# Causal attention: two query groups of equal work and four column tiles instead of two query halves and two column tiles

## The reference

```python
Q, K, V = (proj(Wq, bq), proj(Wk, bk), proj(Wv, bv))
scores = jnp.einsum('bhqd,bhkd->bhqk', Q, K) / scale
scores = jnp.where(causal[None, None], -jnp.inf, scores)
attn = jax.nn.softmax(scores, axis=-1)
ctx = jnp.einsum('bhqk,bhkd->bhqd', attn, V)
out = jnp.einsum('bsd,ed->bse', ctx, Wo) + bo
```

## Time and profile before

| | us |
|---|---|
| median of 3 runs | 1139.42 |
| lowest, highest | 1137.17, 1140.31 |
| the profiled execution | 1135.98 |
| its span, first to last instruction | 1134.4 |

### The profile page before, as it was taken

One profiled execution on the slowest core, in us unless ns is written; L12 is line 12 of the kernel. 1 busy time (PEld: TensorE's weight loads), 2 busy tenths in 40 slices (PEclk: granted clock), 3 DMA queues, 4 the chain that ended last, 5 costly groups with the idle time before them and its releaser, 6 DMA issues.

```text
span 1134.4 us, 18322 instructions
## 1 busy us (share of the span) xinstructions
PE 864.2 (76%) x6048; PEld 506.0 (45%) x6049; DVE 552.8 (49%) x1051; ACT 387.5 (34%) x627; POOL 490.1 (43%) x538
## 2 busy tenths in 40 slices
PE   3199917277978847994689999758688855899995
PEld 1056603122222223662457777523334433577774
DVE  5623345467686352335513333458489755233334
ACT  3322202044455412221145555226402121555551
POOL 2228848888810021212234443123588731444431
PEclk9999957588798967996579999859899975899997
DMA  8224335655510010102843333230000044434323
GB/s 299 68 61 121 114 99 183 207 169 179 174 37 13 2 38 24 34 19 71 323 133 120 130 119 107 93 125 1 0 1 0 1 193 172 142 116 134 116 88 126
DMA packets 45580, 117.72 MB, mean 104 GB/s; under 512 B 10273, under 2 KB 23346, under 8 KB 44626
## 3 DMA queue, kind: packets, MB, share of 16 engines
q0 software_dynamic: 19280, 69.09, 19.1%
q1 hardware_dynamic: 21634, 43.64, 10.8%
q10 hardware_dynamic: 4608, 4.20, 1.1%
HBM read 90.16 MB, written 26.74 MB: 103 GB/s over the span
## 4 chain that ended last, share of the span: by engine, by line
PE 62%; DVE 15%; DMA 8%; POOL 5%; ACT 5%; issue 4%; SPq 1%; ACTq 0%; DVEq 0%; POOLq 0%
PE psum L490 18%; PE psum L518 13%; PE psum L1178 6%; PE psum L502 5%; PE psum L1638 4%; DVE mem L1272 2%; PE psum L174 2%; DMA mem<-w2l_dram 2%; PE psum L1153 2%; POOL mem L222 2%; DVE XTl L143 1%; PE psum L473 1%; PE psum L1665 1%; DMA max_dram<-mem 1%; ACT XTh L164 1%
## 5 line engine op out<-in xcount | busy, mean ns | idle before, releaser
L490 PE MATMUL psum<-mem 128*128 x984 | 233.3, 392 | 6.0 <-ACT psum L587 5.6
L518 PE MATMUL psum<-mem 128*128 x1536 | 178.2, 273 | 4.7 <-DVE mem L730 4.7
L518 PEld LDWEIGHTS psum<-mem 128*128 128x128 f16 x1536 | 149.9, 98 | 23.2 <-issue 5.6
L490 PEld LDWEIGHTS psum<-mem 128*128 128x128 f16 x984 | 98.8, 100 | 116.4 <-issue 20.4
L800 POOL DMA_INDIRECT y_dram<-mem x64 | 63.8, 997 | 164.5 <-DVE mem L738 161.7
L795 POOL DMA_INDIRECT mem<-xn_dram,mem x64 | 64.8, 1013 | 127.0 <-PE psum L473 109.5
L1230 ACT ACTIVATE mem<-psum 128x512 f32<-128x512 f32 (+1 forms) x160 | 80.0, 552 | 110.7 <-PE psum L1161 66.6
L1272 DVE TENSOR_REDUCE mem<-psum 128x2 f32<-128x1024 f32 (+2 forms) x96 | 89.1, 951 | 58.4 <-PE psum L1131 36.4
L730 DVE TENSOR_TENSOR mem<-psum,mem 128x512 f16<-128x512 f32 x128 | 82.4, 686 | 56.1 <-ACT mem L599 56.1
L719 DVE TENSOR_TENSOR mem<-psum,mem 128x256 f16<-128x256 f32 x64 | 27.1, 423 | 160.8 <-ACT mem L581 160.8
L174 PE MATMUL psum<-ident,mem 128*128 128x128 f32 x96 | 32.5, 441 | 95.3 <-DVE mem L148 95.3
(11 more groups left out here) (242 smaller groups left out, 1403.5 us busy)
## 6 DMA issues: line engine op xcount, KB each, us to landing
stage<-in_w POOLq DMA_DIRECT2D x20, 480.0 KB, 4.7
stage<-in_w POOLq DMA_DIRECT2D x16, 512.0 KB, 3.9
w2h_dram<-mem POOLq DMA_DIRECT2D x20, 240.0 KB, 2.9
w2l_dram<-mem POOLq DMA_DIRECT2D x20, 240.0 KB, 3.9
xn_dram<-mem ACTq DMA_DIRECT2D x32, 128.0 KB, 6.5
mem<-w2h_dram SPq DMA_DIRECT2D x2, 2048.0 KB, 13.3
mem<-w2l_dram SPq DMA_DIRECT2D x2, 2048.0 KB, 17.9
mem<-y_dram SPq DMA_DIRECT2D x16, 256.0 KB, 5.2
```

Source lines behind the costliest of these rows:

```text
L490: ins = eng.matmul(out, a[:, p, k, :], w[:, at], start=(gated and i == 0), stop=(i == 3 * KD - 1), skip_group_check=not gated)
L518: ins = eng.matmul(c.bank(6)[:, 0:D], a[:, q * half + j, :], w[:, at], start=(i == 0), stop=(i == 3 * CF - 1))
```

## The change

- The query tiles form two groups, `GROUPS = ((0, 3, 4, 7), (1, 2, 5, 6))`. Each has 18 of the 36 blocks of 128 by 128 below and on the diagonal. The query stack holds the tokens in the order of the groups (`PLACE`), which PE's projection of `wq` sets by a permuted window on its moving operand (`tokens`), and which is undone when `X` is added to (`u = GROUPS[s][t]`). The stage's output order of tiles changes with it.
- A pair has five steps. Each computes scores of both groups (`scores(p, i, y)`, `S_KEYS`), so four activations, then the product of the step before for two heads and two groups, in the four column tiles of bank 7. The widths of the pieces add up to those of before; the ring `pt` has two places of four instead of four of two.
- Maxima are made seven steps ahead (`M_LEAD`), with one piece between the two groups' scores and the rest behind them. Before the loop PE makes all twelve of pair 0 and five of pair 1.
- `max_rows` issues four DMAs per half instead of two, half as large, and `scores(p, 0, 0)` waits for both halves at once (`s_mr[p % 2]`).
- `normalise(p-1)` stands in step 1 of pair p, and its turning back is a part of its own (`turn_back`) in step 2 behind two maxima.
- `wk` is projected before `wq`; the stores of the first six are waited for alone; SP loads `stacks(0)` then, ahead of the stores of `e = 1`, and ACT issues the loads of pairs 1 and 2.
- POOL waits for the first scores (`s_st(1)`) before it starts on `w2`.

```diff
+GROUPS = ((0, 3, 4, 7), (1, 2, 5, 6))
+PLACE = {t: 4 * y + i for y, tiles in enumerate(GROUPS) for i, t in enumerate(tiles)}
+S_KEYS = (((0,), (1, 7), (2, 6), (3, 5), (4,)), ((0,), (1,), (2, 6), (3, 4), (5,)))
+NM, NS = len(M_PIECES), len(S_KEYS[0])
+M_STEPS = (3, 2, 3, 2, 2)
+M_LEAD = 7
...
+def query_span(k, y):
+    n = sum(t >= k for t in GROUPS[y])
+    return (4 * y + 4 - n) * P, n * P
+
+def maxima_at(g):
+    out, at = [], 0
+    p, i = divmod(g + M_LEAD, NS)
+    if 0 <= p < PAIRS:
+        at = sum(M_STEPS[:i])
+        out = [(p, n) for n in range(at, at + M_STEPS[i])]
+    return out
...
-    STACKS, RING, LAG = 3, 4, 2
+    STACKS, RING = 3, 2
...
-    PROJ = [(m, e, s) for e in range(KD) for m in ("wq", "wk") for s in range(T // BANK)]
+    PROJ = [(m, e, s) for e in range(KD) for m in ("wk", "wq") for s in range(T // BANK)]
...
             for j in range(2):
-                row = qs[64 * j + MAX_ROW:64 * j + MAX_ROW + 1, p % STACKS, s * BANK:(s + 1) * BANK]
-                eng.dma_start(row.rearrange("o (u b r) -> o u b r", u=HALF, b=4), rows[j:j + 1, 0:HALF])\
-                    .then_inc(s_mr[s].sem, 16)
+                row = qs[64 * j + MAX_ROW:64 * j + MAX_ROW + 1, p % STACKS, :]
+                row = row.rearrange("o (y g t b r) -> o y g t b r", y=2, g=2, t=2, b=4)
+                for y in range(2):
+                    eng.dma_start(row[:, y, s], rows[j:j + 1, y]).then_inc(s_mr[p % 2].sem, 16)
...
+            if e == 0:
+                eng.wait_ge(*s_pd[0](16 * 6))
+                eng.wait_ge(*s_m(1))
+                stacks(eng, 0)
+        eng.wait_ge(*s_pd[1](16 * 6))
         for p in range(PAIRS):
             for s in range(2):
                 max_rows(p, s)
             if p and p + STACKS - 1 < PAIRS:
-                eng.wait_ge(*s_st(2 * NS * p))
-                stacks(p + STACKS - 1)
+                eng.wait_ge(*s_st(4 * NS * p))
+                stacks(eng, p + STACKS - 1)
...
-        def scores(p, i):
+        def scores(p, i, y):
-            slot, at = p % STACKS, (p * NS + i) * 2
-            if i == 0:
-                eng.wait_ge(*s_mr[0](32 * (p + 1)))
-            if i == 3:
-                eng.wait_ge(*s_mr[1](32 * (p + 1)))
+            slot, at = p % STACKS, (p * NS + i) * 4 + 2 * y
+            if i == 0 and y == 0:
+                eng.wait_ge(*s_mr[p % 2](128 * (p // 2 + 1)))
...
+            off = [0, 0]
+            for n in range(2):
+                for y in range(2):
+                    if n >= len(S_KEYS[y][i]):
+                        continue
+                    k = S_KEYS[y][i][n]
+                    a, w = query_span(k, y)
+                    for j in range(2):
+                        at = 32 * (2 * y + j)
+                        ins = eng.matmul(c.bank(7)[at:at + VW, a - y * BANK:a - y * BANK + w], va[:, k, 2 * p + j, :],
+                                         pt[:, g % RING, 2 * y + j, off[y]:off[y] + w], start=(k == 0), stop=(k == S_KEYS[y][-1][-1]))
+                        if n == len(S_KEYS[y][i]) - 1:
+                            ins.then_inc(s_pv.sem, 1)
+                    off[y] += w
+
+        for g in range(-M_LEAD, 0):
+            for p, n in maxima_at(g):
+                maxima(p, n)
+        for g in range(PAIRS * NS):
+            p, i = divmod(g, NS)
+            pieces = maxima_at(g)
+            scores(p, i, 0)
+            for q, n in pieces[:1]:
+                maxima(q, n)
+            scores(p, i, 1)
+            for q, n in pieces[1:]:
+                maxima(q, n)
+            if g:
+                product(*divmod(g - 1, NS))
+        product(PAIRS - 1, NS - 1)
...
+        eng.wait_ge(*s_pd[0](16 * 6))
+        eng.wait_ge(*s_m(1))
+        for p in range(1, STACKS):
+            stacks(eng, p)
+        for g in range(PAIRS * NS):
+            if g >= RING:
+                eng.wait_ge(*s_pv(4 * (g - RING + 1)))
...
+        for g in range(PAIRS * NS):
+            p, i = divmod(g, NS)
+            if p and i == 1:
+                normalise(p - 1)
+            pieces = maxima_at(g)
+            for q, n in pieces[:2]:
+                maxima(q, n)
+            if p and i == 2:
+                turn_back(p - 1)
+            for q, n in pieces[2:]:
+                maxima(q, n)
         normalise(PAIRS - 1)
+        turn_back(PAIRS - 1)
...
-                u = t + HALF * s
+                u = GROUPS[s][t]
...
         eng.wait_ge(*stage_free)
+        eng.wait_ge(*s_st(1))
```

More of the change, by code:

```diff
@@ L1009, in attention_stage @@
     s_pl = n("pl", 8)
-    s_pd = n("pd", 16 * 12)
+    s_pd = [n(f"pd{e}", 16 * 6) for e in range(KD)]
     s_v = n("v", NT)
@@ L1018, in attention_stage @@
     s_ms = [n(f"ms{i}", 16 * PAIRS) for i in range(2)]
[L1019 to L1022, removed]
+    s_mr = [n(f"mr{i}", 128 * PAIRS // 2) for i in range(2)]
+    s_st = n("st", PAIRS * NS * 4)
+    s_ex = n("ex", PAIRS * NS * 4)
+    s_pv = n("pv", PAIRS * NS * 4)
     s_tn = n("tn", PAIRS)
@@ L1035, in attention_stage, with stacks @@
     s_xd = c.sem("x_rows", NT)
-    PROJ = [(m, e, s) for e in range(KD) for m in ("wq", "wk") for s in range(T // BANK)]
+    PROJ = [(m, e, s) for e in range(KD) for m in ("wk", "wq") for s in range(T // BANK)]
     ORDER = {"wq": (0, 0, 1), "wk": (0, 1, 0)}
+    def stacks(eng, p):
+        slot = p % STACKS
+        for m, dst in (("wq", qs), ("wk", ks)):
+            for j in range(2):
+                rows = A[m + "_dram"][:, (2 * p + j) * DK:(2 * p + j + 1) * DK, :]
+                eng.dma_start(dst[64 * j:64 * j + QK_ROWS, slot, :], rows).then_inc(s_ld[slot].sem, 16)
     def sync(eng):
@@ L1147, in scores @@
             off = 0
-            for k, s in S_PIECES[i]:
-                a, w = query_span(k, s)
-                diag, last = a == k * P, (k, s) == S_PIECES[i][-1]
+            for k in S_KEYS[y][i]:
+                a, w = query_span(k, y)
+                diag, last = k in GROUPS[y], k == S_KEYS[y][i][-1]
                 for j in range(2):
@@ L1167, in product @@
         def product(p, i):
-            eng.wait_ge(*s_ex((p * NS + i + 1) * 2))
+            g = p * NS + i
+            eng.wait_ge(*s_ex(4 * (g + 1)))
             if i == 0 and p:
                 eng.wait_ge(*s_tn(p))
-            off = 0
-            for k, s in S_PIECES[i]:
-                a, w = query_span(k, s)
-                last = k == S_PIECES[2 if s == 0 else NS - 1][-1][0]
-                for j in range(2):
-                    out = c.bank(7)[32 * (2 * s + j):32 * (2 * s + j) + VW, a - s * BANK:a - s * BANK + w]
-                    ins = eng.matmul(out, va[:, k, 2 * p + j, :], pt[:, (p * NS + i) % RING, j, off:off + w],
-                                     start=(k == 0), stop=last)
-                off += w
@@ L1181, in product @@
-            ins.then_inc(s_pv.sem, 1)
-        for n in range(NM):
-            maxima(0, n)
-        for p in range(PAIRS):
-            m = 0
-            for i in range(NS):
-                scores(p, i)
-                if p + 1 < PAIRS:
-                    for _ in range(M_STEPS[i]):
-                        maxima(p + 1, m)
-                        m += 1
-                if p * NS + i >= LAG:
-                    product(*divmod(p * NS + i - LAG, NS))
-        for i in range(PAIRS * NS - LAG, PAIRS * NS):
-            product(*divmod(i, NS))
+            off = [0, 0]
@@ L1297, in normalise, with turn_back @@
                 .then_inc(s_nt.sem, 1)
+        def turn_back(p):
             if p % 2:
@@ L1372, in attention_stage @@
     return dict(pe=pe, act=act, dve=dve, pool=pool, sync=sync, done=s_xd, count=NT,
-                order=[t + HALF * h for t in range(HALF) for h in range(2)], ready=lambda i: s_xd(i + 1), combine=[],
+                order=[GROUPS[s][t] for t in range(HALF) for s in range(2)], ready=lambda i: s_xd(i + 1), combine=[],
                 w2_stored=[s_ws[p](16 * CHUNKS) for p in range(2)])
```

71 lines of the change are left out of this document (26 added, 45 removed).

## The result

| | changed | before |
|---|---|---|
| median of 16 runs, us | 1133.08 | 1141.19 |
| lowest, highest | 1124.65, 1140.98 | 1134.07, 1149.92 |
| the profiled execution (span) | 1129.17 (1127.6) | 1135.98 (1134.4) |

The ratio is 0.9928, 95% interval 0.9903 to 0.9954: faster by 0.7%, where 2.1% was forecast (1112 us, range 1098 to 1128). The sign was right, the size was not, and the median lies outside the range.

The account below looks back on a forecast made before the run. The old loop was held bound by handing over, PE in front; the new one by SP's row maxima DMAs. Start 9.3 plus loop 17.5 gave 26.8 us off 1136.0, 1109.2; the median 3.4 above, 1112 us, range 1098 to 1128.

Parts of the forecast that it names:

- The start: Ahead of the loop: first score at 223 us instead of 232.3, 9.3 us gained, between 4 and 13.
- PE's step and the products: In the loop: products 3.8 us a pair instead of 7.7, a full step 2.3 us, five steps 11 us.
- Rival (2): Products: the four column tiles go two by two, PE 15 us a pair, 1115 to 1122 us; chance 0.10.
- the sum: Loop from the first score: 16.6 us pair 0, 92.5 pairs 1 to 5, 16.6 pair 6, 12.5 pair 7, together 138.
- The row maxima: In the loop: SP's list of DMAs sets pairs with stacks at 18.5 us, bounds 13.5 and 19.1.
- The last pair: Pair 7, end of the loop: no maxima, four steps of 2.5 us, one of 2.0, a last product, 12.5 us.
- rival (5): Whole loop: nothing comes of it, the stalls only move and a pair stays at 21 us; chance 0.05.
- Rival (1): Maxima's rows in time: DVE sets 16.9 us a pair, loop 130, POOL's 133.5 ends it, 1101 us; chance 0.22.
- Rival (4): PE's clock falls with halved products: at 0.50 about 24 us a pair, 20 us slower, 1160; chance 0.06.
- friction: In the loop: PE's waits for ACT's and DVE's banks starve each other, 2 us a pair more, 1126; chance 0.12.
- POOL's stream: Work on w2 beside the loop: ends 133.5 us after the first score, hidden behind 144.5 with 11 to spare.
- the doubt of a full gain: Products: by the skill's 2.38 times for three column tiles, some 5 us a pair instead of the 3.8 taken.

Follow-up runs that it names:

- e6: Changed kernel with row maxima neither stored nor loaded and scores not lowered by them, their matmuls and reductions kept: 0.979, 1110.6 us.
- e9: Changed kernel with maxima nine steps ahead instead of seven, a fourth stack slot, and SP issuing both halves' stores and the stacks before waiting: 0.9869, 1119.96 us.
- e16: e9 with the maxima pieces per step turned by two places, M_STEPS (2, 2, 3, 2, 3): 0.988, median 1124.05 us.

## Why the forecast failed, step by step

- **The start** was right: first score forecast at 223, measured at 223.6. The working was not quite: PE began the first maxima at 204.6 (203 forecast), but SP stood in its wait for the stores of `e = 1` until 212.5 (13.06 us), for which the working had no term; its 5 us were for the stores of `e = 0`, which landed in 2.52. The wait cost little here: the second half's maxima, due at 215.5, were ready at 217.05 and went out at 218.45, and the way from there took 5.2 us instead of 7. Two errors nearly cancelled.
- **PE's step and the products** were right at full clock: sixteen records of four tiles end within 1.06 us, as did four records of two tiles. Rival (2) is out. At 1.2 GHz it is 1.91 us, and the sum had no step at that clock:

```profile
237.55 1.06 PE L1208 MATMUL psum<-mem 128*17 128x384 f32 x16
...
260.47 1.91 PE L1208 MATMUL psum<-mem 128*17 128x384 f32 x16
```

- **The row maxima, the step that failed.** The place was right (the path "that I hold to set the loop"), its two sizes were not. First, "by step 2 DVE has done seven of the twelve pieces and the normalising, about 9.5 of its 16.5 us": DVE's busy time was taken for elapsed time, and PE's pieces for pieces at full clock. DVE waits for PE between them (26.2 us in the loop for L1159 alone). From a pair's first score until the last of the next pair's maxima was ready to be turned it took 9.9, 10.9 and 11.3 us in the pairs 2, 3 and 5, at a granted clock of 1.00, and 12.7 to 13.1 us in the pairs 0, 1, 4 and 6, at 0.50 to 0.68. The pairs 0, 3, 4 and 6, with the columns of the earlier trace rows:

```profile
223.64:236.62 12.98, 10.79 (x112) 4.60 (x112) 8.80 (x8) 8.25 (x16) 8.36 (x8) 0.68 0.39 122
...
283.85:294.75 10.90, 7.49 (x104) 3.38 (x104) 9.23 (x11) 7.51 (x14) 8.87 (x9) 1.00 0.67 204
303.93:316.94 13.01, 11.63 (x96) 4.29 (x96) 8.17 (x12) 6.51 (x12) 10.69 (x10) 0.50 0.60 185
...
343.81:356.52 12.71, 11.21 (x96) 4.12 (x96) 8.17 (x11) 6.51 (x12) 10.35 (x9) 0.53 0.44 152
```

  So of the some 3.4 us that were missing in pairs 0 and 6, about 1.2 are gaps at full clock and about 2.2 go with the lower clock (an estimate from the means of these rows). These two pairs, which have no stacks ahead of their maxima, take 20.9 and 20.5 us, not 16.6. Second, the out-DMA behind the stacks: 9.0 us in the mean, not 7.7. Pairs 1 to 5 take 19.9, not 18.5. In the sum +4.3, +3.9 and +6.8 us.
- **The last pair**, without maxima, was put at 12.5 us and took 16.4, with products of 1.82 and 1.84 us in its chain: +3.9. Here the clock is most of it. The last two transposes lie 13.63 us apart, at a clock of 0.75; in e6 and in e9 the same work takes 10.99, at 1.00 (the changed kernel, then e6):

```profile
367.07:380.70 13.63, 10.31 (x114) 3.97 (x114) 1.39 (x3) 8.13 (x17) 0.00 (x0) 0.75 0.01 1
...
350.61:361.60 10.99, 7.67 (x114) 3.44 (x114) 1.42 (x3) 8.13 (x17) 2.30 (x3) 1.00 0.13 47
```

  The four add up to the 19 us by which the loop is longer than forecast.
- **Against the old loop.** It had slack on this way, since it asked for rows 512 to 1023 only in step 3 and had half as many issues. The change put both on the path, so the gain of the products (PE's busy time fell) turned into a wait for DMA. That is nearest to rival (5): the stall moved.
- **Rival (1)**, had the rows come in time: forecast 1101 with a loop of 130 us, measured in e6 as 1110.6 and 137.7. **Rival (4)**, a clock of 0.50 throughout, did not come, but the clock fell in stretches (0.50 to 1.00), and the sum carried nothing for it. What it cost was more than friction in pairs 0, 6 and 7; in the pairs with stacks SP's list set the length in this profile. No run holds the clock fixed.
- **POOL's stream** was hidden, as forecast: its last store was issued at 354.4, 26 us ahead of the last transpose.
- **Why e6**, with a lead of seven, gets 0.979, while the same without row maxima and a lead of nine gets 0.987 to 0.988, some 10 us: 7 to 9 of them lie ahead of the first score. From the first maxima to the first score it takes 20.1 and 19.5 us instead of 15.1, for 22 maxima pieces instead of 17, and the rest is mostly the filling of four slots instead of three. **Open** is what the longer lead costs in the loop (137.7 against 146.3 and 142.2): no run separates it from the changes of clock between executions.

## What to carry to other kernels

Before halving an engine's work, list every cycle through which one iteration hands over to the next, DMA round trips too, and give each its length in elapsed time, gaps included: busy time understates when a result is due. Price the steps at both clocks of PE, because an engine with less to do may get the lower one. Where two bounds have nearly one length, removing either shows nothing (0.997 twice here), so leave the whole resource out once to see what lies beneath. Price the parts of a change by themselves; here three edits at the start carried all of it.

## What the runs showed of the hardware

- The same kernel varies with the granted clock between executions: e16 from 1115.1 us at a mean of 0.872 to 1127.4 at 0.854, the changed kernel from 1124.65 at 0.866 to 1140.98 at 0.846. The profiled execution of e9 was 11.2 us above its median, so one profile can mislead by 10 us.
- Less work can lower the clock: the median of the granted clock over all executions was 0.859 in the changed kernel, with four column tiles at a time, and 0.878 with two (0.867 and 0.880 with the lead and the order). The Trainium skill ("TensorE: Matmul & The Clock Gate", "What's actually happening") has the clock depend on how busy TensorE has been; these rows agree. That raising it by idle work gained nothing is what the runs add.
- Four float32 column tiles cost no more than two: 1.06 us for 512 columns each in two passes, against 1.04, thus nearly twice the rate. The Trainium skill ("Measured speedup vs the span model" on the same page) has 2.38 for three tiles; the doubt of a full gain that the prediction took from it did not come true.
- In the changed kernel's loop an 8 KB DMA took 1.4 to 2.7 us without stacks ahead of it and 8.2 to 10.3 us behind four loads of 96 KB on the same queue.
